# A product of constants behind every signalling product of layers 1 and 2 of a graph network

## The reference, cut to what matters

```python
def _sage_layer(x, src, dst, Wl_i, bl_i, Wr_i):
    msg = x[src]
    agg = jax.ops.segment_sum(msg, dst, num_segments=N_NODES)
    cnt = jax.ops.segment_sum(jnp.ones((src.shape[0],), x.dtype), dst, num_segments=N_NODES)
    mean = agg / jnp.clip(cnt, 1.0)[:, None]
    return mean @ Wl_i + bl_i + x @ Wr_i
...
h = x
for i in range(N_LAYERS):          # N_LAYERS = 3
    h = _sage_layer(h, src, dst, Wl[i], bl[i], Wr[i])
    if i < N_LAYERS - 1:
        h = jax.nn.relu(h)
x = _layernorm(x + h)
...
z = jnp.concatenate([x[dst], x[src], edge_attr], axis=-1)
msg = jax.nn.sigmoid(z @ Wf.T + bf) * jax.nn.softplus(z @ Ws.T + bs)
agg = jax.ops.segment_sum(msg, dst, num_segments=n)
```

## Time and profile before

| | us |
|---|---|
| median of 3 runs | 5074.12 (5062.85 to 5076.36) |
| the profiled execution | 5070.49 |
| its span | 5068.7 |
| sums of layer 1 | 151 to 1286 |
| sums of layer 2 | 1335 to 2328 |
| sums of layer 3 | 2376 to 3334 |
| the convolution's loop | 3440 to 4980 |

### The profile page before, as it was taken

One profiled execution on the slowest core, in us unless ns is written; L12 is line 12 of the kernel. 1 busy time (PEld: TensorE's weight loads), 2 busy tenths in 40 slices (PEclk: granted clock), 3 DMA queues, 4 the chain that ended last, 5 costly groups with the idle time before them and its releaser, 6 DMA issues. The chain is left out here.

```text
span 5068.7 us, 71564 instructions
## 1 busy us (share of the span) xinstructions
PE 3148.3 (62%) x16221; PEld 2249.0 (44%) x16222; DVE 2214.6 (44%) x5207; ACT 1220.7 (24%) x1906; POOL 2272.8 (45%) x2399
## 2 busy tenths in 40 slices
PE   4455565666466667454566664566777776777775
PEld 4233343444343444344334444454555554555553
DVE  4533333334341212234533333464565555666667
ACT  1111121120100000001000000034555555565565
POOL 2245555440335554553355545515455444444530
PEclk7677777787677777666777877687888788888887
DMA  3232222221233334212445553133233332222321
GB/s 94 72 126 76 78 75 85 76 72 41 71 98 106 102 101 114 52 39 79 139 148 158 157 150 87 46 100 97 83 86 88 85 85 81 82 84 83 85 65 40
DMA packets 345769, 454.38 MB, mean 90 GB/s; under 512 B 135431, under 2 KB 260386, under 8 KB 342099
## 3 DMA queue, kind: packets, MB, share of 16 engines
q0 software_dynamic: 88624, 207.58, 15.0%
q10 hardware_dynamic: 101984, 181.27, 11.3%
q1 hardware_dynamic: 155092, 64.77, 4.9%
HBM read 357.03 MB, written 101.90 MB: 91 GB/s over the span
## 5 line engine op out<-in xcount | busy, mean ns | idle before, releaser
L719 POOL DMA_INDIRECT shared<-y_dram,idx x1584 | 1502.4, 948 | 1702.1 <-DMA idx<-ea_sb 974.2
L906 PE MATMUL ps<-shared,work 128*128 x4368 | 773.8, 329 | 548.6 <-issue 373.2
L759 POOL DMA_INDIRECT shared<-q_dram,idx x784 | 753.3, 961 | 770.1 <-SPq L615 533.6
L906 PEld LDWEIGHTS ps<-shared,work 128*128 128x128 f32 x4368 | 694.7, 236 | 639.4 <-issue 630.0
L1951 DVE TENSOR_TENSOR acc<-acc,ps 128x129 f32 x546 | 156.5, 287 | 1623.2 <-remote 844.8
L1106 PE MATMUL ps<-pq,work 128*128 x1664 | 592.5, 458 | 147.2 <-issue 45.4
L925 PE MATMUL ps<-pq,work 128*128 128x385 bf16 x1456 | 340.2, 377 | 223.0 <-issue 134.4
L1106 PEld LDWEIGHTS ps<-pq,work 128*128 128x128 f32 x1664 | 304.1, 228 | 260.0 <-issue 205.6
L1885 DVE SCALAR_TENSOR_TENSOR work<-ps,w_of,dstT_sb 128x512 f32<-128x512 f32 x555 | 412.5, 744 | 3.6 <-issue 3.5
L2234 DVE TENSOR_TENSOR work<-ps,shared 128x256 f32<-128x256 f32 x832 | 294.5, 416 | 247.2 <-PE ps L1109 106.8
L1257 ACT CAST work<-ps 128x300 bf16<-128x300 f32 (+1 forms) x520 | 189.2, 406 | 863.3 <-PE ps L897 449.5
(11 more groups left out here) (354 smaller groups left out, 3794.5 us busy)
## 6 DMA issues: line engine op xcount, KB each, us to landing
work<-counts_dram ACTq DMA_DIRECT2D x156, 384.0 KB
counts_dram<-work ACTq DMA_DIRECT2D x26, 1568.0 KB
shared<-y_dram,idx POOLq DMA_INDIRECT x1584
ea_parts<-work ACTq DMA_DIRECT2D x128, 196.0 KB
ea_sb<-ea_parts SPq DMA_DIRECT2D x196, 128.0 KB
work<-counts_dram ACTq DMA_DIRECT2D x52, 416.0 KB
shared<-q_dram,idx POOLq DMA_INDIRECT x784
y_dram<-work SPq DMA_DIRECT2D x21, 448.0 KB, 3.0
```

The source lines that it names most:

```text
L719: pool.indirect_dma_start(msg[:, u, 0:F], None, y_dram, bass.IndirectOffsetOnAxis(ap=idx[:, u:u + 1], axis=0)).then_inc(s_quad[q], 16)
L759: pool.indirect_dma_start(q_ring[:, u * 2 * F:(u + 1) * 2 * F], None, q_dram, bass.IndirectOffsetOnAxis(ap=idx[:, u:u + 1], axis=0)).then_ ...
L906: last = te.matmul(ps[:, SUM_BANKS[i], 0:FA], lhsT=oh4[:, OH_SLOTS[i], u, :], rhs=shared[:, bass.ds(place + u * FA, FA)], start=u == 0, st ...
```

## The change

A function `unread_product` is added to `sage_sums`. In layers 1 and 2 it issues one f32 product of two constants, the identity by the row of numbers 0 to 127, into bank 6, which nobody reads in those layers. It waits for nothing and raises nothing. It is called behind the second product of `count`, and behind the last product of `item`, `multiply`, `multiply_piece` and `pair_item`.

```diff
-DENSE_BANK, COUNT_BANKS = 3, (4, 5)
+DENSE_BANK, COUNT_BANKS, UNREAD_BANK = 3, (4, 5), 6
...
+                def unread_product():
+
+                    if layer < 2:
+                        te.matmul(ps[:, UNREAD_BANK, 0:P], lhsT=ident[:, :], rhs=iota[:, :], start=True, stop=True)
+
                 def count(n, k, slot):
...
                         at += CELLS[h]
+                    unread_product()
...
                     last.then_inc(s["summed"], 1)
+                    unread_product()
...
                 def multiply(it):
...
                     last.then_inc(s["multiplied"], 1)
+                    unread_product()
...
                 def multiply_piece(it, p_):
...
                     last.then_inc(s["counted"], 1)
+                    unread_product()
...
                 def pair_item(turn, i, place):
...
                     last.then_inc(s["multiplied"], 1)
+                    unread_product()
```

## The result

The changed kernel takes 5108.4 us, median of 8 runs (5089.4 to 5131.2), against 5072.7 us for the kernel before, measured beside it (8 runs, 5054.7 to 5100.1): a ratio of **1.0079 [1.0051, 1.0106]**, 40 us slower by the ratio (36 us between the medians), where 141 us was forecast. The sign and most of the parts came as predicted; one term of the sum, the share of the new products that costs time, was far too large.

The account below looks back on a forecast made before the run. Layers 1 and 2 were taken as bound by signals held during gathers (30%) and otherwise by PE's order of work. 750 x 0.27 = 202 us, x 0.70 = 141; 5070.5 + 141 = 5212 us, range 4900 to 5340 (8 in 10).

Parts of the forecast that it names:

- Signals: Layers 1 and 2: signals stay held while gathers run, followed or not; VectorE's remote waits stay about 320 us in each.
- Number and price: Layers 1 and 2: 880 products, 1,760 more PE records, 0.112 us apart at 2.4 GHz; 0.27 us a product.
- Layer 3 and the convolution unchanged: Outside the changed layers: layer 3's sum stays at 958 us, the convolution within a few us.
- Exposed counts: Layer 1's counts: 130 of 260 products are covered by PE's wait for ScalarE's copy, the others are exposed.
- the held share: Layers 1 and 2: products cost nothing in 30% of the time (remote waits, 647 of 2128 us), so 202 x 0.70 = 141 us.
- The exposure in layer 1: Layer 1: 401 of 531 products lie in PE's way, 401 x 0.27 x 0.70 = 76 us.
- the first counts' gap: Layer 1: PE idles 0.38 us between first and second count; the first's product costs nothing there at full clock.
- the clock pays: Layers 1 and 2: more PE work may keep the clock at 2.4 GHz, 133 us less, 5079 us; chance 0.09.
- The signposts: Changed trace: layers 1 and 2 at about 1211 and 1059 us, remote waits about 320 us each, clock below 0.85.
- the freeing case: Layers 1 and 2: the product behind a signal ends its hold; 4918 us if half goes, 4625 if all; chance 0.22.
- the forecast's own range: Whole kernel, if the new products only cost PE's time: 5120 to 5330 us; chance 0.59.

Follow-up runs that it names:

- e7: Unread products behind the pair items alone (126 of the 880), against the kernel before: ratio 0.9986 [0.9961, 1.0011].
- e10: Unread products only in layer 1's pair items (63), plus 30 in PE's idle time before them, against the kernel before: ratio 0.9969 [0.9946, 0.9992].

## Why the prediction was right in kind and wrong in size

By its own steps:

- **Signals.** Right. The remote waits stayed (655 against 647 us), and layer 1 and 2 grew where freed signals would have shortened them. In the runs with copies the holds are gone, so they go with the indirect form of the gathers. How these hold a signal stays open, and since the copies also keep GpSimd busy for less time (265 us in place of 463 in layer 1), what part of the 22% is the holds' is not shown.
- **Number and price.** Right: 1,760 records, at full clock about 0.11 us apart (two in 0.39 us at 1484.18, of which the last lasts 0.275); they last 314 ns in the mean.
- **Layer 3 and the convolution unchanged.** Right within the scatter: 958 to 970 us, and from the last item of layer 3 to the end 1738 to 1748 us, which is 1700 to 1765 over the profiles with indexed gathers.
- **Exposed counts.** I took 130 of the 260 as exposed, 25 us after the held share. The counts cost 12 us alone and 18 by difference, so this was somewhat too much.
- **The held share: a step that failed, shown for layer 2.** I read the share in which the products are free off the adder's remote waits, 30% of the time, and took the other 70% as exposed, "because PE's work in a free stretch is seen to be last". But GpSimd's runs last 622 and 603 us whether PE is idle or busy beside them, held or not. A signal is only late in the later part of a run, so the remote waits (647 us) count half of the time beside gathers (about 1,225 us). Of the new records, 501 of layer 1 and 233 of layer 2 start between runs, 734 of 1,760, or 42% instead of 70%. With that the prediction's own sum is 202 x 0.42 = 85 us in place of 141, a little more than half of the miss. In layer 2 a run settles it: 66 us forecast, 16 measured, 62 with the gathers replaced by copies.
- **The exposure in layer 1: the other step that failed.** I had 401 of 531 products lying in PE's way, 76 us. The layer grew by 20 us, and by 27 with no gather to hide beside, so a larger share beside gathers is not what makes them cheap: most of them cost next to nothing outside it too. In the kernels with copies the 531 products occupy PE for 158 us, while PE's idle time shrinks by 40 us and its useful records occupy it for 91 us less (a record counts up to the start of the next; all of this is worked out from the starts in the trace). Both terms the prediction had at nothing, but for the first counts' gap.
- **The same two terms in the real kernel.** The 734 records between runs occupy PE for 88 and 41 us (0.35 us a product, above my 0.27, which was the distance to a follower). Of those 129 us only about 33 show up. Between the runs of layer 1: 88 us of unread products, less 28 us in which PE had been idle (199 to 171 us), less 40 us by which the useful products there take less (328 to 288 us), is +20 us; in layer 2 41 - 16 - 12 = +13 us. In layer 1 nothing had on balance moved beside a run: 1,562 useful records start between runs before, 1,643 after. Each occupies PE for less, most of all in the pair items (63 to 38 us for the same 252 records). That is the clock in part, and in part that a record with nothing behind it counts to its own end and one with a product right behind it only to that one's start; the two were not sized apart. In layer 2 fewer of the long records of the pieces start between runs (427, then 358), so there it is mostly work that moved beside a run. I had put the idle time only at the first counts, and the clock at nothing, since the gaps in which it falls stay empty. They do, but in work that is broken by short waits it is higher all the same: 0.76 to 0.82 in a layer, 0.59 to 0.87 among the pair items. The Trainium skill ("TensorE: Matmul & The Clock Gate", section "Why this matters for your kernels") advises to keep TensorE busy continuously for the most throughput. These rows bear that out for the clock, but padding for its sake did not make the kernel faster: the pair items became 6.5 us shorter and the whole 40 us longer. Where the padding stands in a stretch of low clock alone (e7) it is free, and whether e10 is a gain is not sure.

The rival "the clock pays" (5079) came closer to the number than my forecast, with a chance of 0.09, and its mechanism is a part of the difference that the trace does not size. The signposts I named pointed the right way: remote waits unchanged, clock up but under 0.85, layers grown by much less than forecast, the case in which "PE's time outside the held stretches was not last". That the range from 4900 held the result is luck: it reached so low only for the freeing case, which did not happen, and the forecast's own range, from 5120, did not hold it.

## What to carry to other kernels

When one engine works through bursts of fixed length, ask what the time beside a burst costs another engine: in layer 2 of this kernel it was nearly free (16 us against 62 without the bursts). The share that is not free is read from the burst engine's own timeline, and not from the waits that the bursts cause. Outside the bursts an engine that is busy 60% of a layer is not "last" all the time either: check each new piece of work against the idle time and the ends of the records that it follows. Here padding TensorE cost at first less than its steady price (40 us, then 88 to 90 us for every further 880 products), as it filled idle time and raised the granted clock. If it is tried, then in a stretch of low clock, and with full products: a padding of one column was worse than one of 128.

## What the hardware showed that was not expected

- With 528 plain copies per layer in place of 528 indirect gathers of the same size, the layers shrink from 1148, 931 and 951 us to 789, 568 and 644 us, and the whole by 22%; the adder's 844.8 us of remote waits vanish. VectorE waits for such a signal for up to 18.3 us beside GpSimd's indirect gathers, and beside as many plain copies from the same queue not at all. How much of the 22% is these waits, and how much that GpSimd is busy for a shorter time (265 to 268 us a layer in place of 463 to 483), is not shown; no edit of TensorE's queue that was tried frees the signals.
- A hold sets in with the length of the run. In layers 1 and 2 of the trace of before, worked out from the ends of the items and the next semaphore event, 12 of 61 signals in the first 2 us of a run are late by over 0.6 us, 81 of 120 at 2 to 6 us and 61 of 64 beyond; between runs 109 of 119 take under 0.15 us and none over 2.6. (One event in ten is missing from the trace, so the shares are rough.)
- In layer 1 products of one column lower the granted clock below what empty places leave: 0.50 against 0.59 among the pair items, 0.69 against 0.78 in the turns. In layer 2 they do not (0.77 against 0.74).
